# A transformer block on one core: PSUM banks of the first attention shared out anew, and the combines of the last experts moved

## The reference, cut to what matters

```
x = x + attn_a(layernorm(x))     # 16 heads of 8 channels, rotary, causal, softmax, projection
x = x + ffn(layernorm(x))        # top 4 of 64 experts, per token
x = x + attn_b(layernorm(x))     # one head of 128 channels; scores times a band mask of 64, softmax
x = x + ffn(layernorm(x))        # the same experts again

ffn:  sel = sigmoid(xf @ expert_sel.T);  sel_val, sel_idx = top_k(sel, 4)
      h = einsum('nd,kde->nke', xf, keys)
      out = einsum('nke,kev->nv', relu(h) * gates[:, :, None], values)
```

## Time and profile before

| | |
|---|---|
| median of 3 runs | 1338.33 us (1334.89 to 1345.9) |
| the profiled execution | 1334.34 us |
| its span | 1332.4 us |
| PE, DVE, ACT, POOL busy | 877.1, 808.2, 484.9, 836.1 us |
| first attention, up to its last exponential | about 480 us |
| from the first gather of layer 1 to the end | 1121.5 to 1332.4 us |

### The profile page before, as it was taken

One profiled execution on the slowest core, in us unless ns is written; L12 is line 12 of the kernel. 1 busy time (PEld: TensorE's weight loads), 2 busy tenths in 40 slices (PEclk: granted clock), 3 DMA queues, 4 the chain that ended last, 5 costly groups with the idle time before them and its releaser, 6 DMA issues.

```text
span 1332.4 us, 20381 instructions
## 1 busy us (share of the span) xinstructions
PE 877.1 (66%) x6298; PEld 601.8 (45%) x6298; DVE 808.2 (61%) x2325; ACT 484.9 (36%) x1249; POOL 836.1 (63%) x1023
## 2 busy tenths in 40 slices
PE   1999988988899658798776453423288756964100
PEld 0334433333344227798675332313177756864100
DVE  2677888798887424664674874635586752653212
ACT  1156646565455513364443211101134323542000
POOL 5234647879766766287982647556367473996575
PEclk9999989999898858898897665555678887987655
DMA  6555533332261334587563101012125544863321
GB/s 191 200 193 198 190 125 119 97 94 95 70 213 54 90 104 118 153 243 223 165 168 91 45 28 51 35 37 84 31 72 163 153 143 121 239 182 114 100 68 53
DMA packets 206537, 163.67 MB, mean 123 GB/s; under 512 B 15968, under 2 KB 191072, under 8 KB 206432
## 3 DMA queue, kind: packets, MB, share of 16 engines
q1 hardware_dynamic: 185696, 112.00, 29.3%
q0 software_dynamic: 16384, 33.59, 7.9%
q10 hardware_dynamic: 4352, 16.78, 3.3%
HBM read 78.94 MB, written 83.36 MB: 122 GB/s over the span
## 4 chain that ended last, share of the span: by engine, by line
PE 34%; DVE 30%; POOL 14%; issue 11%; another core or an unknown queue 6%; DMA 2%; SPq 2%; ACT 1%; POOLq 0%; DVEq 0%; ACTq 0%
POOL v_aug L1621 8%; PE ps L697 6%; PE ps L706 5%; PE ps L600 5%; PE ps L538 4%; DVE x_res L1322 3%; PE ps L579 3%; PE ps L686 3%; PE ps L565 3%; DVE row_max L1096 2%; POOL w_attn L1604 2%; DVE st L1040 1%; DVE block_max L1096 1%; DVE dest_f L1291 1%
## 5 line engine op out<-in xcount | busy, mean ns | idle before, releaser
L1608 POOL DMA_INDIRECT sorted_rows<-xn,dest x256 | 253.2, 989 | 166.6 <-DVE dest L1295 107.2
L1621 POOL DMA_INDIRECT v_aug<-result_rows,dest x256 | 245.5, 959 | 132.1 <-issue 64.9
L883 ACT ACTIVATE arena<-ps 128x512 f32<-128x512 f32 x320 | 182.7, 605 | 105.9 <-PE ps L538 98.0
L697 PE MATMUL ps<-arena 128*128 128x128 f32 x1024 | 153.8, 299 | 54.8 <-DVE arena L1307 30.8
L565 PE MATMUL ps<-arena 64*128 64x128 bf16 (+3 forms) x576 | 142.8, 311 | 39.9 <-DMA arena<-k_parts 16.9
L872 ACT COPY arena<-ps 128x512 f32<-128x512 f32 x128 | 75.0, 586 | 254.3 <-PE ps L706 160.9
L697 PEld LDWEIGHTS ps<-arena 128*128 128x128 f32 x1024 | 140.1, 212 | 60.7 <-DVE arena L1307 32.9
L1307 DVE COPY arena<-ps 128x512 f32<-128x512 f32 x128 | 88.1, 689 | 125.6 <-PE ps L686 77.0
L706 PE MATMUL ps<-arena 128*128 x1024 | 148.2, 292 | 18.0 <-ACT arena L872 7.7
L1096 DVE TENSOR_REDUCE row_max<-ps 128x1 f32<-128x512 f32 (+1 forms) x192 | 128.9, 684 | 42.5 <-PE ps L579 39.8
L706 PEld LDWEIGHTS ps<-arena 128*128 128x128 f32 x1024 | 136.7, 208 | 20.0 <-issue 19.9
(11 more groups left out here) (190 smaller groups left out, 1302.9 us busy)
## 6 DMA issues: line engine op xcount, KB each, us to landing
arena<-sorted_rows SPq DMA_DIRECT2D x128, 256.0 KB
result_rows<-arena SPq DMA_DIRECT2D x128, 256.0 KB
sorted_rows<-arena ACTq DMA_DIRECT2D x16, 1024.0 KB, 4.4
arena<-q_parts SPq DMA_DIRECT2D x16, 512.0 KB
arena<-k_parts SPq DMA_DIRECT2D x16, 512.0 KB
q_parts<-parts SPq DMA_DIRECT2D x52, 128.0 KB, 2.8
k_parts<-parts SPq DMA_DIRECT2D x50, 128.0 KB, 2.9
sorted_rows<-xn,dest POOLq DMA_INDIRECT x256
```

The lines of the kernel that those rows point to most:

```text
L697: mm = pe.matmul(ps[:, e_bank(2, layer, half, n), P * i:P * i + P], ktile[:, v, P * i:P * i + P], xtt[:, v, P * i:P * i + P], start=True, ...
L883: nc.scalar.activation(prob[:, grp % 2, pr % 2, PROB_AT[u]:PROB_AT[u] + T], ps[:, v % 3, :], ACT.Exp, scale=SCALE_A).then_inc(exp_done, 1)
L1608: g.indirect_dma_start(sorted_d[b // HALF][:, :], bass.IndirectOffsetOnAxis(dest[:, 16 * b + n:16 * b + n + 1], 0), xn1[:, b % 2, n // TOP ...
L1621: g.indirect_dma_start(yg[:, b % 2, i // TOPK, C * c:C * c + C], None, result_d[layer][b // HALF][:, :], bass.IndirectOffsetOnAxis(dest[:, ...
```

## The change

1. First attention: the tiles for ACT get two banks (0 and 1) and those for DVE four (2 to 5). PE waits for exponential v-2 instead of v-3, and for maximum n-4 instead of n-3. No instruction is added, removed or moved there.
2. Last expert steps: `COMBINE_AT = (13, 26)`. Batch 0 is combined behind step 13 instead of 12, batch 1 behind step 26 instead of 19. Batches 2 and 3 are combined behind the last step.
3. Batch 2 of the last gathers is no longer paced.
4. The last batch is combined and written out in two halves of two token tiles, with a semaphore of its own (`yg_last`) for the second half's fetches.

```diff
-COMBINE_AT = (12, 19, 26, 33)
+COMBINE_AT = (13, 26)
...
-            for b in range(B):
-                sp.wait_ge(combined, 16 * (B + b + 1))
-                sp.dma_start(out_d.rearrange("(t p) c -> p t c", p=P)[:, TT * b:TT * b + TT, :],
-                             x[:, TT * b:TT * b + TT, :]).then_inc(done_out, 16)
-            sp.wait_ge(done_out, 16 * B)
+            for half in range(2 * B):
+                if half % 2 or half >= 2 * B - 2:
+                    lo = TT * (half // 2) if half < 2 * B - 2 else 2 * half
+                    sp.wait_ge(combined, 16 * B + 8 * (half + 1))
+                    sp.dma_start(out_d.rearrange("(t p) c -> p t c", p=P)[:, lo:2 * half + 2, :], x[:, lo:2 * half + 2, :]).then_inc(done_out, 16)
+            sp.wait_ge(done_out, 16 * (B + 1))
...
-                if v >= 3:
-                    pe.wait_ge(exp_done, v - 2)
+                if v >= 2:
+                    pe.wait_ge(exp_done, v - 1)
...
-                    return pe.matmul(ps[:, v % 3, at:at + n], kk[rows, s, pair, P * j:P * j + P], qs[rows, s, pair, P * j:T],
+                    return pe.matmul(ps[:, v % 2, at:at + n], kk[rows, s, pair, P * j:P * j + P], qs[rows, s, pair, P * j:T],
...
-                if n >= 3:
-                    pe.wait_ge(s1_free, n - 2)
-                bank = ps[:, 3 + n % 3, :]
+                if n >= 4:
+                    pe.wait_ge(s1_free, n - 3)
+                bank = ps[:, 2 + n % 4, :]
...
+            def combine_part(part):
+                b = B - 1
+                n = B + b
+                if part:
+                    dve.wait_ge(yg_last, 128)
+                else:
+                    dve.wait_ge(yg_in[b % 2], 256 * (n // 2) + 128)
+                for c in range(TOPK):
+                    dve.wait_ge(combined, 16 * n + 8 * part + 2 * c)
+                    for t in (2 * part, 2 * part + 1):
...
-            for b in range(HALF, B):
+            for b in range(len(COMBINE_AT), B - 1):
                 combine(1, b)
+            for part in range(2):
+                combine_part(part)
...
-                gather(1, b, paced=b < HALF - 1)
+                gather(1, b, paced=b < 2)
```

More of the change, by code:

```diff
@@ L359, in build @@
         yg_in = [sem(f"yg_in{i}") for i in range(2)]
+        yg_last = sem("yg_last")
         combined = sem("combined")
@@ L882, in _ @@
                         act.wait_ge(s2_ready, v + 1)
-                        nc.scalar.activation(prob[:, grp % 2, pr % 2, PROB_AT[u]:PROB_AT[u] + T], ps[:, v % 3, :], ACT.Exp,
+                        nc.scalar.activation(prob[:, grp % 2, pr % 2, PROB_AT[u]:PROB_AT[u] + T], ps[:, v % 2, :], ACT.Exp,
                                              scale=SCALE_A).then_inc(exp_done, 1)
@@ L1320, in combine @@
                     for t in range(TT):
+                        xt = x[:, TT * b + t, :]
+                        nc.vector.scalar_tensor_tensor(out=xt, in0=yg[:, b % 2, t, C * c:C * c + C],
+                                                       scalar=top[:, TT * b + t, c:c + 1], in1=xt,
+                                                       op0=ALU.mult, op1=ALU.add).then_inc(combined, 1)
+            def combine_part(part):
[8 more added lines that the diff above has]
+                    for t in (2 * part, 2 * part + 1):
                         xt = x[:, TT * b + t, :]
@@ L1619, in gather @@
                 for i in range(lo, hi):
-                    c = i % TOPK
+                    c, late = i % TOPK, (layer, b) == (1, B - 1) and i >= TT * TOPK // 2
                     g.indirect_dma_start(yg[:, b % 2, i // TOPK, C * c:C * c + C], None, result_d[layer][b // HALF][:, :],
-                                         bass.IndirectOffsetOnAxis(dest[:, 16 * b + i:16 * b + i + 1], 0)).then_inc(yg_in[b % 2], 16)
+                                         bass.IndirectOffsetOnAxis(dest[:, 16 * b + i:16 * b + i + 1], 0)
+                                         ).then_inc(yg_last if late else yg_in[b % 2], 16)
                     if paced:
```

## The result

| | before | after |
|---|---|---|
| median | 1337.11 us (1331.97 to 1345.9, 20 runs) | 1344.05 us (1337.12 to 1352.69, 20 runs) |
| ratio, 95% interval | | 1.0042 [1.0025, 1.0059] |
| profiled execution, its span | 1334.34, 1332.4 us | 1337.12, 1335.4 us |
| last exponential of the first attention starts | 478.1 us | 483.3 us |
| first gather of layer 1 to the end | 210.9 us | 208.7 us |

The change made the kernel a little slower, 0.4%, where 1.2% faster was forecast. (1344.05 us also lies outside the range of 1306 to 1342.) The two halves of the table point apart: the end is 2.2 us shorter, the attention 5.2 us longer, where 14.1 shorter was forecast. (Between them lies code that the change doesn't touch.)

A forecast was written before the change was run, and what follows sets the result against it. The prediction saw a chain of waits that no engine rules. Gains of 14.1 (attention) + 0 (last expert steps) + 2.3 (halving) = 16.4 us took the profiled 1334.3 to 1317.9, from the median 1322 us; range 1306 to 1342.

The forecast's parts named there:

- Sum for the attention: First attention: five iterations gain 3.35 us each, one 0.85, less 1.0 and 2.5: 14.1 us gained.
- The stops for maxima: First attention, slots 4 and 5: with four banks PE's 3.22 us of standing per iteration falls to 1.1, 2.1 gained.
- the clock's 1.7 us: First attention, behind the stop at slot 5: no fall of PE's clock expected, worth 1.7 us of PE work an iteration.
- Two banks for the exponentials: First attention: PE waits longer for ACT, costing 0.45 us an iteration, about 1 in iteration 0 and 2.5 in iteration 7.
- the stop of 2.29 us: First attention, slot 5: PE stands 2.29 us for a bank DVE has not emptied, DVE said to work without a gap.
- the two stretches in the earlier trace: Two other unpaced batches beside which DVE also stands, free again at 711.6 and 1104.9, 3 us behind the last transfer.
- DVE is the wall: Rival, first attention: DVE's work limits it, the fourth bank buys nothing and only the halving stays: 1336 us, chance 0.22.
- ACT cannot keep up: Rival, first attention: with two banks PE waits for ACT, deciding from 2 us an iteration on: 1352 us, chance 0.08.
- The last expert steps: End of the kernel: 20.1 us of removed waits and combine go into standing beside unpaced batch 2, net gain 0.
- no standing: Rival, end of the kernel: engines do not stand beside unpaced transfers, batch 4 starts at 1218 instead of 1241: 1299 us, chance 0.04.
- The halving: End of the kernel: the last batch combined and written in two halves shortens the last combine and write, 2.3 us gained.

The follow-up runs named there:

- e12: The changed kernel run again unaltered, in a series where the kernel before takes about 1226 us: 1215.98 us, 0.9899 of the kernel before.
- e14: The kernel before with only the new end (old three and three banks), in a series where the kernel before takes about 1226 us: 1211.67 us, 0.9871 of it.
- e4: The changed kernel with the old three and three banks, so only the end is new: 0.9984 of the kernel before.
- e1: The kernel before with only the new banks (two for exponentials, four for maxima) and the old end: 1.0011 of the kernel before.
- e2: As e1, but from iteration 3 SP waits for the scatter transfers before the slot 4 loads of queries and keys: 0.9935 of the kernel before.
- e13: The changed kernel plus SP's wait for the scatter before the 1 MB load and the expert weights, batch 2 unpaced: 1200.3 us, 0.9786 of the kernel before.
- e7: The changed kernel plus SP's wait for the scatter (also before the expert weights), batch 2 paced: 1323.66 us, 0.9832 of the kernel before.
- e5: The kernel before with the new end, but batch 2 of the last gathers paced again, old banks: 0.9885 of the kernel before.
- e3: The kernel before with two banks for the exponentials, three for the maxima and one unused: 1.0062 of the kernel before.
- e15: As e1, run again in a series where the kernel before takes about 1226 us: 1230.08 us, 1.0023 of the kernel before.
- e9: The kernel before; from iteration 3 slot 4's loads wait for a 512-wide maximum, ahead of the maxima's write, to meet the scatter: 1226.94 us, 0.9992 of the kernel before.
- e8: The kernel before with the slot 4 loads of queries and keys issued on SP ahead of the maxima's rows: 1.0023 of the kernel before.

## Why the prediction was wrong

**The step that failed is "Sum for the attention: five iterations at 2.1 + 1.7 - 0.45 = 3.35 ...: 14.1 us gained".** Instead of 14.1 us gained, 5.2 us were lost (10.5 in the later series, e12 against e14; by the timed ratios 0.6 and 0.3% against the same kernel without the banks, e4 and e14). It has three errors in it, in the order of their weight.

- *What the lead triggers.* The stops for maxima went as forecast, and iteration 2 gained 4 us (1 us in e1 and e2). But I followed PE's lead only to PE's and DVE's next steps, and cost the transfers that MROW0 releases at nothing. SP had waited there, and its next item is 1 MB. Moved ahead of the last scatter it makes POOL's norm 2 to 4 us late in three of five iterations, which takes PE's lead, and the clock falls around NT. Shown by e1 and e2, which differ by one wait: 13.9 us in the profiles, 10 by the ratios. With the wait the attention is 7.9 us shorter than before (e2), 4.9 in the later series (e13 against e14); by the ratios 7 to 10 (e2; e7 against e5; e13 against e14). That is a third to three quarters of my 14.1.
- *That the clock's 1.7 us would simply be kept.* They are 8.5 of the 14.1 us. In the changed kernel the clock fell behind the short stop all the same, and around NT too: PEclk over 55 us went from 0.94 to 0.85. With SP's wait (e2) it stays at 1.00 behind the same stop of 1.27 us (248 to 252 us), but at the iteration's start (222 to 238 us) it is at 0.68 instead of 0.89, and from 100 to 470 us at 0.92, as before (0.90 in the changed kernel). So this term brought nothing in either kernel. Why the clock falls behind 1.27 us in one kernel and not in the other stays open.
- *Two banks for the exponentials.* 5.8 us in my sum; about 8 by e3's timed ratio. PE's waits for ACT rose by 4.2 us, 14 of them up to 1.0 us, where I had said below 0.5. How the price divides between ACT and DVE with four banks beside it stays open.

Where PE's lead goes when the load is held back, e2's waits say (100 to 480 us): ACT 5.9 us, POOL 9.8 (the norm 4.1, the masked exponentials of line 1660 5.7), and once 4.0 for DVE at MROW0, against 5.0 that are left of the 22.5 for the maxima. An engine that is let go at one place meets the next one at another.

Two readings of the prediction were inexact and change nothing in its sum. DVE does not work without a gap at the stop of 2.29 us: it idles 0.91 us before 247.44. And of the two stretches in the earlier trace rows the second (1082.2 to 1102.2) lies beside unpaced scatters of rows, not gathers.

The rivals. *DVE is the wall* asked for a fourth bank that buys nothing; e2 and e13 show that it buys 5 to 8 us net by the profiles, and DVE worked less, not more (41.1 of 55 us). *ACT cannot keep up* had the right sign and the wrong mechanism; its condition, 2 us an iteration, was not met (6.1 us in seven). None of the rivals was a transfer that comes too early. In the profile of before it could be read: scatter at 252.60, load at 254.74, norm at 254.92 after a wait of 0.26 us for the scatter, all within 2.4 us of each other in the very stretch whose order the change moves.

**The last expert steps, costed at 0, were right in the first series** and for the reason given: two stretches of standing, and batch 4 starts 118.2 us behind the first gather in the changed kernel and 120.8 in e4, where 119.8 was forecast. That the whole end, with the halving, gained 2.2 us where 2.3 were forecast is luck in part: in e4, with the same end, it gained 0.3. e5 shows the other side of the same sum: paced, the vanished waits are worth 14.4 us. The rival *no standing*, which I gave 0.04, is what the later series do: batch 4 starts 96.6 us behind the first gather in e12, 109.4 in e15, and the end is 15 us shorter (I had worked out 23, against a kernel before that stands). The Trainium skill's rule on turns packet by packet (DMA: Bandwidth & Descriptors, Queues, rings and completion order) agrees with e12, where 16 unpaced transfers stop nobody; in the first series the standing of 7.13, 7.09, 7.84 and 6.34 us goes beyond it. For the scatter inside the load the rule gives the direction in both: its packets, which had 1 MB of others beside them, started up to 5.6 us behind the issue instead of 1.7.

**The halving** was right in size where engines don't stand: 2.5 us against 2.3. In the first series the time from the last transfer's issue to the end is 9.9 to 10.1 us whole, and halved 8.4 (e4), 9.2 (the change), 10.3 (e5) and 10.5 (e7), so that no gain is shown there. In the changed kernel's own profile it gave 0.7, since DVE stood once more inside the last eight instructions and 3.7 us, instead of 2.2 in e12, passed from the last of them to the end.

## What to carry to other kernels

When a change lets an engine run ahead, list what that engine's jobs release on the transfer queues, and look for small latency-bound transfers (here a scatter that a norm waits for) within a few us of a large load that now starts earlier; a wait that holds the load back can be worth more than the buffer that made it early. A lateness costs nothing as long as its consumer is behind (e9) and most of itself once the consumer has been freed: price slack and lead together. Don't add the clock to a gain from a shorter stop before a run has shown it. And an answer that hangs on engines standing without a visible cause should be tested in more than one series of runs, on different chips where that can be had.

## What was not expected of the hardware

- An indirect scatter, issued 1.3 us behind the second of two 512 KB loads, landed after 6.3 us (after 4.3 at the same distance in e9); issued ahead of the load, it let the norm start 2.3 us after its issue; issued 3.9 us behind the load (e8) it was not late at all.
- The same program took 1226 us in two series of runs and 1337 to 1345 in three others, with DVE busy for the same time (808.2 us before, 807.8 in e9, which differs from it by one wait and one move on SP). In the slower ones DVE stands for up to 13.9 us at a time (e5, at 960) beside back-to-back indirect transfers, PE and ACT stand there too, and the profile knows no releaser ("remote", "issue"). Beside transfers with 0.65 us of memset between them the longest of DVE's stops is 3.0 us in the profiles of before, the change and e5. What the engines lack in that time is open. That they wait for their own instructions is not borne out: in the profile of before no packet that fetches instructions starts between 1202.2 and 1232.0, while DVE goes on at 1223.9 and 1228.8.
- The clock fell to half behind a stop of 2.29 us (0.57 in 250 to 254 us before) and behind one of 1.27 us (0.57 in 248 to 252 after), but not behind the same 1.27 us in e2 (1.00).
